# A scan kernel on one core: the scan's input from fp16 pairs of x and of B times the difference matrix, one projection for dt, B and C, and C in two parts

## What is computed

```
x = x + 0.5 * ffn(layernorm(x))      # "A" pass
x = x + ssm(layernorm(x))            # "S" stage
x = x + 0.5 * ffn(layernorm(x))      # "C" pass

ffn(x):  gate, up = fp4_linear(x, w_gate), fp4_linear(x, w_up)       # 256 -> 704
         return fp4_linear(silu(gate) * up, w_down)                  # 704 -> 256
         # fp4_linear rounds both operands in blocks of 16 to an 8-value grid times a scale

ssm(x):  BC = x @ W_in + b_in;  B, C = BC[..., :16], BC[..., 16:]
         dt = clip(softplus((x @ W_dt1 + b_dt1) @ W_dt2 + b_dt2), 1e-7, 1e6)     # 64 between
         a  = exp(A * dt)                                  # A is [256 channels, 16 states]
         b  = expm1(A * dt) / (A * dt) * dt * B * x
         h[t] = a[t] * h[t-1] + b[t]                       # 512 tokens, 256 channels x 16 states
         return sum_n(h * C) + D * x
```

## Time and profile before

| | before |
|---|---|
| median of 3 runs | 4263.15 us (4262.46 to 4264.17) |
| profiled execution, device time | 4264.34 us |
| profiled execution, span of the records | 4262.6 us |
| PE busy | 3955.9 us, 93% |
| DVE busy | 3769.4 us, 88% |
| ACT busy | 3303.1 us, 77% |
| POOL busy | 1605.2 us, 38% |
| one iteration of the loop | 126.6 us |

### The profile page before, as it was taken

One profiled execution on the slowest core, in us unless ns is written; L12 is line 12 of the kernel. 1 busy time (PEld: TensorE's weight loads), 2 busy tenths in 40 slices (PEclk: granted clock), 3 DMA queues, 4 the chain that ended last, 5 costly groups with the idle time before them and its releaser, 6 DMA issues. The chain is left out here.

```text
span 4262.6 us, 73878 instructions
## 1 busy us (share of the span) xinstructions
PE 3955.9 (93%) x26156; PEld 3065.0 (72%) x26156; DVE 3769.4 (88%) x6378; ACT 3303.1 (77%) x6053; POOL 1605.2 (38%) x1230
## 2 busy tenths in 40 slices
...
GB/s 28 10 11 16 6 16 11 16 16 16 6 16 11 16 16 16 16 6 15 12 16 16 16 6 16 11 16 16 16 15 8 11 16 16 16 16 6 11 11 10
DMA packets 47540, 57.49 MB, mean 13 GB/s; under 512 B 8583, under 2 KB 42824, under 8 KB 47176
## 3 DMA queue, kind: packets, MB, share of 16 engines
...
## 5 line engine op out<-in xcount | busy, mean ns | idle before, releaser
L717 DVE TENSOR_TENSOR_SCAN state<-w_ps,decay 128x512 f32<-128x512 f32 x1024 | 1210.5, 1211 | 28.2 <-PE w_ps L1109 20.7
L1109 PE MATMUL w_ps<-dif,bx 128*128 128x129 f32 (+1 forms) x8192 | 1087.6, 281 | 30.3 <-DVE c_state L710 23.7
L1040 PE MATMUL gu_ps<-wgu,qxT 128*128 128x352 f16 x6144 | 1050.1, 324 | 63.2 <-DVE hid L640 49.9
L1109 PEld LDWEIGHTS w_ps<-dif,bx 128*128 128x128 f32 x8192 | 1017.1, 196 | 110.5 <-issue 91.6
L1040 PEld LDWEIGHTS gu_ps<-wgu,qxT 128*128 128x128 f16 x6144 | 607.6, 101 | 431.6 <-DVE hid L640 73.0
L911 ACT ACTIVATE bx<-s_xh,B_tok 128x256 f32<-128x256 f32 x2048 | 862.1, 498 | 18.0 <-DVE B_tok L678 16.9
L727 DVE SCALAR_TENSOR_TENSOR c_state<-state,inv_A,rep_ps 128x512 f32<-128x512 f32 x1024 | 722.4, 737 | 30.7 <-PE rep_ps L1118 20.4
L1047 PE MATMUL td_ps<-wd,qhT 128*128 128x256 f32 x3072 | 727.5, 387 | 20.1 <-ACT qhT L844 20.1
L421 POOL TENSOR_TENSOR val<-val,magic 128x704 f32<-128x704 f32 x256 | 409.4, 1599 | 886.5 <-DVE magic L660 886.5
L920 ACT ACTIVATE decay<-dt,A_sb 128x512 f32<-128x512 f32 x1024 | 691.1, 714 | 5.0 <-DVE state L717 2.4
L1047 PEld LDWEIGHTS td_ps<-wd,qhT 128*128 128x128 f32 x3072 | 569.9, 192 | 121.1 <-ACT qhT L844 36.8
...
## 6 DMA issues: line engine op xcount, KB each, us to landing
...
b_C<-in_L_attn_b_in SPq DMA_DIRECT2D x5, 0.1 KB
...
```

The costliest lines, as they stand in the source:

```text
L717: v.tensor_tensor_scan(state[:, n % 2, gi, :], w_ps[:, gi, :], decay[:, n % 2, gi, :], 0.0, ALU.add, ALU.mult).then_inc(state_ready.sem, 1)
L1040: last = te.matmul(gu_ps[:, m, 0:FH], qxT[:, t // 2, 4 * (t % 2) + xp * G + c], wgu[:, c, wp, a:a + FH], start=begin, stop=end)
L1109: last = te.matmul(w_ps[:, gi, t * P:t * P + wide], bx[:, n % 2, t, gi * P:(gi + 1) * P], dif[:, 0:wide], start=t == 0, stop=t == T - 1, s ...
```

## The change

The scan's input w is made with the operands' roles changed. `x_parts` holds the normalised x of a sequence as two fp16 tiles (high part by ACT, `high_x`; rest by POOL, `low_x`), and is the stationary operand for all n. For each n, the constant `dif` (now fp16) is scaled by B: ACT writes the high part (`high_b`, 4 instructions of 128x129, where `times_b` had 4 of 128x256), POOL the low part (`low_b`, one instruction of 128x4x129). `differences` then issues three fp16 matmuls (high-high, high-low, low-high) where it had one fp32 matmul. The product tile `bdif` has 4 buffers.

dt, B and C come from one projection with 112 output rows (`project`, 2 fp32 matmuls of 512 columns), taken by one ACT instruction (`take_rBC`). `project_C` and `project_B` go; B with tokens on partitions comes from 4 transposes of 16 rows (`transpose_B`), which wait for `take_rBC`. `take_B` is three DVE instructions. C has two fp16 parts, each written by one DVE instruction from PSUM. A power-of-two scale for B and C is found at the start (`bc_*`), and the norm of stage S carries a factor 2^10. The constant DMAs are 16. All four lists in `ORDER` are new; PE's, ACT's and POOL's preamble stand below.

```diff
 ORDER = {
     "PE": """
-    A.gu0 A.gu1 A.gu2 S.xt0 A.gu3 S.bt0 S.cm0 S.rb0 A.gu4 S.z0 S.k0 S.k1 S.w0 A.gu5 S.c0 S.w1 S.e0 S.e1 A.ht0
-    A.gu6 A.ht1 A.gu7 ...
+    A.gu0 A.gu1 A.gu2 S.xt0 A.gu3 S.rb0 S.bt0 A.gu4 A.gu5 S.z0 S.k0 S.k1 S.w0 S.w1 S.c0 A.gu6 A.gu7 A.ht0 S.e0
+    S.e1 A.ht1 ...
     "ACT": """
-    A.gu0 A.gu1 S.ln0 A.gu2 C.ln0 S.xt0 A.gu3 C.ax0 S.b0 S.b1 S.cm0 S.rb0 A.gu4 C.ax1 A.ah0 S.z0 A.gu5 A.ah1 ...
+    A.gu0 A.gu1 S.ln0 A.gu2 C.ln0 S.xt0 A.gu3 S.xh0 C.ax0 S.rb0 C.ax1 A.gu4 S.b0 S.b1 A.gu5 A.ah0 S.z0 A.gu6 ...
     "POOL": """
-    S.ln0 C.ln0 C.mx0 A.mv0 A.mv1 A.mh0 A.mh1 C.mx1 A.mv2 A.mv3 A.mh2 A.mh3 C.mv0 C.mv1 C.mh0 C.mh1 C.mv2 C.mv3
-    N.ln0 C.mh2 C.mh3 N.mx0 N.mx1
+    S.ln0 C.ln0 C.mx0 A.mv0 A.mv1 S.xl0 S.bl0 S.bl1 A.mh0 A.mh1 S.bl2 S.bl3 C.mx1 A.mv2 A.mv3 S.bl4 S.bl5 S.bl6
+    A.mh2 A.mh3 S.bl7 S.bl8 S.bl9 C.mv0 C.mv1 C.mh0 C.mh1 S.bl10 S.bl11 S.bl12 S.bl13 C.mv2 S.bl14 C.mh2 C.mv3
+    N.ln0 C.mh3 S.bl15 N.mx0 N.mx1
...
+        x_parts = sb("x_parts", [P, 2, T, DM], F16)
+        B_hi = sb("B_hi", [P, T, N], F16)
         B_tok = sb("B_tok", [P, T, N])
+        B_lo = sb("B_lo", [P, T, N], F16)
-        bx = sb("bx", [P, 2, T, DM])
+        bdif = sb("bdif", [P, NB, T, 2, WIDE], F16)
...
+            def low_x(seq):
+                pool.wait_ge(x_hi.sem, x_hi.at(seq, 1))
+                g.tensor_tensor(x_parts[:, 1], s_xh[:], x_parts[:, 0], ALU.subtract).then_inc(x_lo.sem, 1)
+
+            def low_b(seq, n):
+                if n == 0:
+                    pool.wait_ge(B_ready.sem, B_ready.at(seq, 3))
+                if n >= NB:
+                    pool.wait_ge(w_ready.sem, w_ready.at(seq, G + G * (n - NB + 1)))
+                ...
+                g.tensor_tensor(bdif[:, n % NB, :, 1, 0:P + 1], dif[:, 0:P + 1].unsqueeze(1).broadcast_to([P, T, P + 1]),
+                                B_lo[:, :, n:n + 1].broadcast_to([P, T, P + 1]), ALU.mult).then_inc(b_lo_ready.sem, 1)
...
             def take_B(seq):
-                v.tensor_tensor(B_tok[:], w_ps[:, 0, 0:T * N].rearrange("p (t n) -> p t n", t=T),
-                                b_B[:].unsqueeze(1).broadcast_to([P, T, N]), ALU.add).then_inc(B_ready.sem, 1)
+                v.tensor_copy(B_hi[:], B_bank).then_inc(B_ready.sem, 1)
+                dve.wait_ge(B_ready.sem, B_ready.at(seq, 1))
+                v.tensor_copy(B_tok[:], B_hi[:]).then_inc(B_ready.sem, 1)
+                v.tensor_tensor(B_lo[:], B_bank, B_hi[:], ALU.subtract).then_inc(B_ready.sem, 1)
...
             def split_C(seq):
-                v.tensor_copy(C_parts[:], C_ch[0:K3, :]).then_inc(C_step.sem, 1)
-                v.tensor_tensor(C_rest[:], C_ch[0:2 * N, :], C_parts[0:2 * N, :], ALU.subtract).then_inc(C_step.sem, 1)
-                v.tensor_copy(C_parts[0:2 * N, :], C_rest[:]).then_inc(C_step.sem, 1)
-                v.tensor_tensor(C_rest[0:N, :], C_rest[0:N, :], C_parts[0:N, :], ALU.subtract).then_inc(C_step.sem, 1)
-                v.tensor_copy(C_parts[0:N, :], C_rest[0:N, :]).then_inc(C_step.sem, 1)
+                v.tensor_scalar(C_parts[0:N, :], y_ps[ROW_C:PR, 0, :], b_C[0:N, :], None,
+                                ALU.add).then_inc(C_step.sem, 1)
+                v.scalar_tensor_tensor(C_parts[2 * N:KC, :], y_ps[ROW_C:PR, 0, :], b_C[0:N, :], C_parts[0:N, :],
+                                       ALU.add, ALU.subtract).then_inc(C_step.sem, 1)
...
+            def high_x(seq):
+                ...
+                a.copy(x_parts[:, 0], s_xh[:]).then_inc(x_hi.sem, 1)
-            def times_b(seq, n):
+            def high_b(seq, n):
...
                 for t in range(T):
-                    last = a.activation(bx[:, n % 2, t, :], s_xh[:, t, :], ACT.Copy, scale=B_tok[:, t, n:n + 1])
-                last.then_inc(bx_ready.sem, 1)
+                    last = a.activation(bdif[:, n % NB, t, 0, 0:P + 1], dif[:, 0:P + 1], ACT.Copy,
+                                        scale=B_tok[:, t, n:n + 1])
+                last.then_inc(b_hi_ready.sem, 1)
...
+            def project(seq):
+                    last = te.matmul(y_ps[0:PR, 0, :], W_rBC[:, gi, :], xT[:, gi, :], start=gi == 0, stop=gi == G - 1)
-            def project_C(seq): ...
-            def project_B(seq): ...
+            def transpose_B(seq):
+                pe.wait_ge(r_ready.sem, r_ready.at(seq, 1))
                 for t in range(T):
+                    last = te.transpose(w_ps[:, 0, t * N:(t + 1) * N], rBC[ROW_B:ROW_B + N, t * P:(t + 1) * P],
+                                        ident[ROW_B:ROW_B + N, ROW_B:ROW_B + N])
...
             def differences(seq, m):
                 n, gi = m // G, m % G
-                pe.wait_ge(bx_ready.sem, bx_ready.at(seq, n + 1))
+                if n == 0 and gi == 0:
+                    pe.wait_ge(x_lo.sem, x_lo.at(seq, 1))
+                pe.wait_ge(b_hi_ready.sem, b_hi_ready.at(seq, n + 1))
+                pe.wait_ge(b_lo_ready.sem, b_lo_ready.at(seq, n + 1))
...
                 for t in range(T):
                     wide = P + (t < T - 1)
-                    last = te.matmul(w_ps[:, gi, t * P:t * P + wide], bx[:, n % 2, t, gi * P:(gi + 1) * P],
-                                     dif[:, 0:wide], start=t == 0, stop=t == T - 1, skip_group_check=True)
+                    for xp, bp in PARTS:
+                        last = te.matmul(w_ps[:, gi, t * P:t * P + wide], x_parts[:, xp, t, gi * P:(gi + 1) * P],
+                                         bdif[:, n % NB, t, bp, 0:wide], start=(t, xp, bp) == (0, 0, 0),
+                                         stop=(t, xp) == (T - 1, 1), skip_group_check=True)
```

282 lines of the change are left out of this document (161 added, 121 removed).

## The result

| | before | after |
|---|---|---|
| median | 4263.06 us of 4 runs (4262.46 to 4264.17) | 4115.6 us of 4 runs (4113.18 to 4118.5) |
| ratio | | 0.9654, 95% interval 0.9637 to 0.9671 |
| profiled execution, its span | 4264.34, 4262.6 us | 4118.5, 4116.8 us |
| one iteration of the loop | 126.6 us | 121.7 us |

What follows compares the result with a forecast made beforehand. PE was taken as the bound, DVE 3.3 us behind in the middle. DVE work 114.2, collisions 2.5 and idle 10.5 less 5.8 make 122.5 us an iteration against 126.6, so 4132 us; own case 4070 to 4200, 8 in 10 3970 to 4310.

Steps and rivals of the forecast that it cites:

- The new matmuls: PE's difference matmuls: 55 ns each, 0.66 us a piece, saving 0.23 us a piece and 7.4 us an iteration.
- Rivals 3 and 4: PE's difference matmuls: at 79 ns, 4219 us, chance 0.10; or fp16 weight loads show in full, 4488 us, chance 0.02.
- The bound leaves PE: Middle of the iteration: PE no longer busy 70.0 of 70.0 us, and DVE above 94% there.
- The three waits of the earlier trace put down to PE: DVE before scans, products and a feed-forward instruction: waits for PE shrink from 6.1 us an iteration to about 2.
- PE's wait at `transpose_B`: Preamble: PE waits some 1.2 us for ACT's `take_rBC`, covered by the 1.8 us of `project_C` no longer preceding dt.
- DVE's work and collisions: DVE over an iteration: 114.2 us of work, plus 2.5 us of waiting for POOL at the shared port.
- DVE's idle time: DVE over an iteration: 10.5 us of idle time falls by 5.8: 2.2 preamble, 2.0 middle, 0.5 elsewhere.
- the 2.83 us wait of the earlier trace: Preamble: DVE's wait for a gate/up group in the low clock loses 2.2 us, as no group stands there.
- this chain: Preamble, projection to dt: if longer, the forecast is wrong; each us dt comes later is a us of DVE idle.
- ACT, POOL, the clock: ACT some 99.5 us an iteration, scalings near 390 ns; POOL some 70 us; low clock not spreading beyond 6.5 us.
- Rival 1: DVE: no port collisions and idle time falls to 4.4 us; 118.6 us an iteration, 4008 us; chance 0.18.
- Rival 2: Quantisation chain of DVE and POOL: collisions 5.4 us, DVE idle stays 10.5; 130.1 us an iteration, 4376 us; chance 0.19.

Runs made afterwards that it cites:

- Run 1: Kernel after with the product of x's low part and B's high part left out, two fp16 products in each difference instead of three: 4098.29 us.
- run 2: Kernel after with a fourth product (low x times low B) added to each difference: 4269.34 us, ratio to before 1.0016.
- runs 3 and 4: One extra 128-element DVE reduction after every second scan, 16 an iteration: in the kernel after 4159.35 us, in the kernel before 4294.47 us.
- run 5: Kernel after with POOL's low part of B written for one token tile of four, except the first four pieces of the first sequence: 4103.96 us.
- Run 7: Kernel after with the feed-forward pieces A.hid5 and A.am2 moved ahead of the two direct products in DVE's list: 4115.73 us.
- run 12: Kernel after with the preamble's DVE, ACT and POOL lists reordered so that dt should come earlier: 4257.62 us.
- run 9: One projection and C in two parts, the scan's input from one fp32 product as before, in the lists of the kernel before: 4248.72 us, ratio 0.9968.
- the projection half alone: One projection and C in two parts, without the fp16 difference products: 4275.83 us in the lists of after, 4248.72 us in those of before.
- run 6: Kernel after with each of POOL's 16 `low_b` pieces issued twice, the second time to a spare tile: 4214.78 us.
- runs 10 and 11: Whole change with PE's, DVE's and ACT's lists as before: 4413.37 us; the same with C.mv3 and N.ln0 moved earlier in POOL's list: 4242.08 us.

## Why the prediction was right, step by step

**The new matmuls: right.** 55 ns was taken from eight transposes of the earlier trace rows; 57 ns came. 0.685 us a piece, not 0.66, makes 0.8 us an iteration, most of the distance between the predicted 112.0 us of PE and the measured 113.25. Rivals 3 and 4 (79 and 101 ns) are out. The 81 ns that the Trainium skill ("TensorE: Matmul & The Clock Gate", section "Back-to-back issue gap") gives for such a stream disagrees with the 57 ns of 24 matmuls with a weight load each.

**The bound leaves PE: right, and shown. It goes to DVE: right for the middle, not for the whole.** PE is 64.95 of 66 us in the middle and DVE 65.07, 99%. Run 1 shows that less PE work is worth a ninth, run 2 that more of it costs at once. Of DVE's work runs 3 and 4 show only a weak contrast, and in runs 5 and 7 it falls by 37 and 28 us for 12 and 0 us of time. By these rows the kernel after is held by DVE in the middle and by the chain to dt in the preamble. The three waits of the earlier trace rows put down to PE went from 6.1 us an iteration to 46.9 / 32 = 1.5, where about 2 was forecast.

**PE's wait at `transpose_B`: right.** 36.0 us / 32 = 1.1 us, and 1.2 was forecast.

**DVE's work and collisions: right in sum, sizes off.** The sum had 114.2 of work and 2.5 of collisions, 116.7; the iteration has 114.49. The groups of the lines that stretch, before and then after:

```profile
L660 DVE TENSOR_SCALAR magic<-magic 128x704 bf16<-128x704 bf16 x256 | 86.4, 338 | 10.6 <-ACT magic L854 10.6
L619 DVE TENSOR_SCALAR x_magic<-x_magic 128x512 bf16<-128x512 bf16 x128 | 46.0, 360 | 1.5 <-ACT x_magic L850 1.5
```

```profile
L737 DVE TENSOR_SCALAR magic<-magic 128x704 bf16<-128x704 bf16 x256 | 109.6, 428 | 9.2 <-ACT magic L930 9.0
L696 DVE TENSOR_SCALAR x_magic<-x_magic 128x512 bf16<-128x512 bf16 x128 | 67.4, 547 | 1.5 <-ACT x_magic L926 1.5
```

L737 gained 90 ns on 8 instructions an iteration, L696 187 on 4, L743 65 on 8: 2.0 us; L733 (266 to 206 ns) and the scale before it lost some 60 ns each on 4, -0.5. That is 1.5 us of collisions, not 2.5, which agrees with run 5 (37 us / 32 = 1.2 for 333 of the 596 us of new POOL work). And on the path it is less again: 12 of 37 us. The forecast took each collision as lost time, while those of the preamble fall where DVE would wait. The new C and B instructions save 1.7 us an iteration by their groups (118.8 + 7.3 us of them before, 48.1 + 22.2 after); 1.9, with bounds 1.2 and 2.5, was forecast. Together that is 0.2 us less, and the iteration shows 1.6 less: most of the rest is not work but the measure. Records of neighbouring instructions overlap where DVE doesn't wait between them, and busy time counts the overlap once; over 23 iterations the durations themselves sum to 127.9 us an iteration before and 127.8 after.
That one of the two engines holds the port for a whole instruction, as the Trainium skill has it ("SBUF — State Buffer", section "Who interferes with whom"), agrees with run 12: 2.11 us for a cast of 0.20 us, beside a POOL instruction of 2.12.

**DVE's idle time: the step that failed.** 5.8 us was forecast and 7.2 measured. Of the 2.83 us wait of the earlier trace rows, 2.2 were to go since no gate/up group would stand in the low clock. The wait went, though not for that reason: gate/up groups 6 and 7 start in the low clock, which ends at 2017, and take 5.04 us where one group takes 1.95 at clock 1.00, and DVE's list has other work there. A new wait came, 91.4 us / 32 = 2.9 us before `direct`. DVE arrives there earlier by what the split of C saves, and finds PE not done. Run 7 shows that it isn't the place in the list but the chain to dt, run 9 that the projection half alone makes it. The chain itself is in PE's timeline, before and after:

```profile
1948.49 1.98 PE L1088 MATMUL y_ps<-rT,W_dt_sb 64*128 64x512 f32 x4 [0.19 <-ACT rT L876]
```

```profile
2007.12 1.98 PE L1160 MATMUL y_ps<-rBC,W_dt_sb 64*128 64x512 f32 x4
...
2015.01 5.04 PE L1120 MATMUL gu_ps<-wgu,qxT 128*128 128x352 f16 x24
```

Counted from the start of the stage's statistics (1931.76 and 1989.40), the projection for dt starts 3.5 us earlier than before (12.9 to 9.3), and z, behind two gate/up groups, 1.0 us later (16.7 to 17.7), as does dt (25.6 to 26.6). So the 1.8 us of `project_C`, which by the forecast covered the wait at `transpose_B` for dt, didn't reach dt. The prediction named this chain as what could make it wrong, and gave it no term. Against that stand two gains that it didn't price: the quantised tile's wait for POOL, 47.7 to 10.1 us (1.2 us an iteration), and `CB`'s, 31.1 to 3.5 us (0.9). They don't need the new lists: in run 9, in the lists of before, these waits are 14.9 and 3.5 us.
So the sum, 122.5 against 121.7 us, is closer than its terms, and that is luck: idle time 1.4 too low, work and collisions together 2.2 too high. It is one iteration; over 23 of them DVE is busy 114.6 us and idles 7.0.

**ACT, POOL, the clock: right.** ACT 99.51 us (99.5 forecast); its scalings 397 ns (near 390); POOL 66.97 (70), with 1056 ns for a `low_b` and 2124 for `low_x` (1.1 and 2.1 us). The fall of the clock stays as short as in the earlier trace rows: 0.50 from 2011 to 2017 here, and over the run a granted clock of 0.970 for 0.965 before. One reading of the code was off and changed nothing: with four buffers `low_b` for n waits for the differences of n-4, not n-3.

```profile
L989 ACT ACTIVATE bdif<-dif,B_tok 128x129 f16<-128x129 f16 x2048 | 642.4, 397 | 18.9 <-DVE B_tok L759 18.9
L437 POOL TENSOR_TENSOR bdif<-dif,B_lo 128x516 f16<-128x516 f16 x512 | 528.0, 1056 | 31.7 <-PE w_ps L1186 31.5 <-DVE B_lo L760 0.3
```

```profile
2011.00:2012.00 1.00, 0.29 (x4) 0.23 (x4) 0.88 (x2) 0.99 (x1) 1.00 (x2) 0.50 0.00 0
...
2017.00:2018.00 1.00, 1.00 (x6) 0.57 (x5) 0.86 (x2) 0.99 (x3) 0.00 (x0) 0.68 0.00 0
```

**The rivals.** Rival 1 needed DVE's idle time to fall to 4.4 us; it stayed at 7.2, and run 5, with over half of the new POOL work gone, still takes 4104 us and not 4008. Rival 2 was to decide at 12.4 us of collisions and idle time; they are 8.7 (1.5 + 7.2). Its mechanism showed where it was forced: on POOL in run 6, and through the lists in runs 10 and 11.

**What the prediction underrated: the lists.** It treated the four new lists as the frame in which the operations' savings would land. The runs say otherwise. The fp16 product on top of the projection half is worth 160 us in the lists of after (4275.83 to 4115.6) and 7 us in those of before with POOL's mended (4248.72 to 4242.08). The new operations without fitting lists give 21 us of the 147. Neither number is "the lists' share" by itself: operations and order pay together, and with the order the granted clock changes too (0.970 in the lists of after, 0.953 in run 11). Which of the order's other moves carry the rest of run 11's 126 us, beside A.qp0's place (90 us by its group) and the gate/up waits (50 us), is open; other waits are shorter there, so the two don't simply add.
